# A two-layer graph network on one core: groups of 1,024 edges handled two at a time in the second layer and in the target scores of the first

## What is computed

```python
# layer 0 (per edge: src, dst; per head)
xl    = x @ W_lin.T
alpha = leaky_relu(xl[dst]*att_src + xl[src]*att_dst + (edge_attr_16 @ W_edge.T)*att_edge, 0.2)
e     = exp(alpha - segment_max(alpha, dst)[dst])
out   = segment_sum(xl[src] * e / segment_sum(e, dst)[dst], dst) + bias + x
x     = layernorm(x + elu(layernorm(out) * gamma + beta))
# layer 1
q, k, v = x @ Wq.T, x @ Wk.T, x @ Wv.T
alpha = sum_over_head(q[dst] * edge_attr_128 * k[src]) / sqrt(16) * edge_weight1
x     = layernorm(x + segment_sum(alpha * v[src], dst))
```

## Time and profile before

| what | us |
|---|---|
| median of 3 runs | 4161.83 (4160.66 to 4164.23) |
| the profiled execution | 4163.54 |
| its span, first to last instruction | 4161.8 |
| POOL busy | 3065.4 (74%) |
| DVE busy | 2682.8 (64%) |
| PE busy | 1924.6 (46%) |

### The profile page before, as it was taken

How to read it: one execution, slowest core, us unless ns; L and a number is a source line. 1 busy time by engine, 2 the same in 40 slices (tenths; PEclk the granted TensorE clock), 3 DMA queues, 4 the chain that set the end, 5 groups by cost and what they waited for, 6 DMA issues and landing times.

```text
span 4161.8 us, 47315 instructions
## 1 busy us (share of the span) xinstructions
PE 1924.6 (46%) x10576; PEld 1610.4 (39%) x10576; DVE 2682.8 (64%) x5083; ACT 256.5 (6%) x646; POOL 3065.4 (74%) x3247
## 2 busy tenths in 40 slices
PE   4644444554443454444534444444444444444444
PEld 2433333433332343333424444444444444444444
DVE  3555555655555566555657777777777777777776
ACT  1101101100111110001100000000000000000000
POOL 7777777777777777777447777777777777777775
PEclk6666667667666777766755555555555555555555
DMA  8444444444444444444257676666767767677674
GB/s 207 135 133 120 113 129 140 128 140 125 121 120 120 140 132 136 125 127 117 80 183 220 212 218 218 218 220 214 222 208 221 219 214 223 215 217 219 211 224 148
DMA packets 374070, 711.11 MB, mean 171 GB/s; under 512 B 129715, under 2 KB 217780, under 8 KB 373764
## 3 DMA queue, kind: packets, MB, share of 16 engines
q0 software_dynamic: 129504, 324.46, 28.8%
q1 hardware_dynamic: 198040, 354.75, 26.4%
q10 hardware_dynamic: 46476, 31.39, 2.4%
HBM read 682.18 MB, written 28.15 MB: 171 GB/s over the span
## 4 chain that ended last, share of the span: by engine, by line
POOL 37%; issue 21%; DVE 17%; DVEq 9%; PE 8%; DMA 5%; ACT 2%; POOLq 0%; SPq 0%; ACTq 0%
POOL ring L1326 23%; POOL ring L575 14%; DVEq L912 4%; DVE work L915 4%; DMA ring<-kv_table,den_cols 3%; PE psum L1352 3%; PE psum L697 2%; DVE psum L1468 1%; DVE ring L1466 1%; DVE psum L1463 1%; DVE ring L1477 1%; DVEq L73 1%; DMA dst_all<-dst_row_dram 1%; DVE work L1012 0%; DVE work L1015 0%
## 5 line engine op out<-in xcount | busy, mean ns | idle before, releaser
L575 POOL DMA_INDIRECT ring<-x_table,idx x1584 | 1501.0, 948 | 482.6 <-issue 459.7
L1326 POOL DMA_INDIRECT ring<-kv_table,den_cols x1516 | 1434.0, 946 | 462.1 <-issue 447.4
L1352 PE MATMUL psum<-work,ring 128*128 128x42 f32 x3232 | 735.3, 420 | 1093.0 <-DVE ring L1477 1093.0
L1352 PEld LDWEIGHTS psum<-work,ring 128*128 128x128 f32 x3232 | 704.5, 330 | 1148.6 <-DVE ring L1477 1148.6
L697 PE MATMUL psum<-work 128*42 128x132 f32 x3232 | 483.4, 312 | 201.5 <-DVE work L1015 201.4
L697 PEld LDWEIGHTS psum<-work 128*42 128x42 f32 x3232 | 407.0, 135 | 256.9 <-DVE work L1015 233.7
L1463 DVE TENSOR_TENSOR psum<-psum,ring 128x1024 f32<-128x1024 f32 x202 | 248.3, 1229 | 328.8 <-DMA ring<-kv_table,den_cols 304.0
L915 DVE TENSOR_TENSOR work<-dst_all,psum 126x1024 bf16<-126x1024 int32 x204 | 249.1, 1221 | 74.1 <-issue 42.9
L1453 DVE TENSOR_TENSOR work<-dst_all,psum 126x1024 bf16<-126x1024 int32 x202 | 246.7, 1221 | 77.8 <-issue 68.2
L1466 DVE TENSOR_TENSOR ring<-psum,ring 128x1024 f32<-128x1024 f32 x202 | 247.4, 1225 | 20.8 <-issue 9.5
L1468 DVE TENSOR_REDUCE psum<-ring 128x64 f32<-128x1024 f32 x202 | 247.9, 1227 | 14.8
(11 more groups left out here) (201 smaller groups left out, 2125.2 us busy)
## 6 DMA issues: line engine op xcount, KB each, us to landing
dst_all<-dst_row_dram SPq DMA_DIRECT2D x406, 512.0 KB, 5.7
ring<-ea_dram SPq DMA_DIRECT2D x202, 512.0 KB, 4.0
ring<-x_table,idx POOLq DMA_INDIRECT x1584
ring<-kv_table,den_cols POOLq DMA_INDIRECT x1516, 2.8
ea_pair<-ea_turned_dram SPq DMA_DIRECT2D x102, 128.0 KB
kv_table<-work ACTq DMA_DIRECT2D x17, 512.0 KB, 3.1
q_table<-work ACTq DMA_DIRECT2D x17, 384.0 KB, 3.9
ring<-q_table SPq DMA_DIRECT2D x202, 31.5 KB
```

Source lines behind the costliest of these rows:

```text
L575: pool.indirect_dma_start(x_rows[:, h * CHUNK_TILES + t, :], None, k["x_table"], bass.IndirectOffsetOnAxis(idx[h][:, t:t + 1], 0))\
L1326: pool.indirect_dma_start(kv[j][:, t, :], None, k["kv_table"], bass.IndirectOffsetOnAxis(index[:, tile:tile + 1], 0))\
L1352: last = pe.matmul(sum_ps[j % 2], message[j % 2][:, t, :], onehot[j][:, t, :], start=t == 0, stop=t == GROUP - 1)
```

## The change

Layer 0: `dst_all` of two buffers becomes one tensor `dst_pair`; one DMA loads 1 MB for two groups, one DVE instruction compares both, and the node numbers of all 12 groups of a chunk are made by one instruction ahead of the chunk (`first_nodes`). There is one such buffer and one `onehotT`, each for two groups.

Layer 1: all work goes in steps of two groups (16 tiles): DVE instructions over 2,048 columns, one wait for each two groups, three buffers of key/value rows of 16 tiles, two of `w` and `q_win`, one of `dst_pair`, `onehotT` and `q_ps`. The compare for two steps ahead stands after the messages, the adds of the step before stand between the products. Sums of a step are 16 matmuls; the two window bases are read once a chunk into registers.

```diff
-    dst_all = [sb(f"dst_all{i}", [P, GROUP * P], I32) for i in range(2)]
+    dst_pair = sb("dst_pair", [P, 2 * GROUP * P], I32)
+    dst_all = [dst_pair[:, i * GROUP * P:(i + 1) * GROUP * P] for i in range(2)]
...
-    onehotT = [part(GP // 2).bitcast(BF16)[0:KWIN, :] for _ in range(2)]
+    onehotT = part(GP).bitcast(BF16)[0:KWIN, :]
...
                         starts = window_starts(sp, regs, k["base_sb"], first_group, r)
+                        sp.wait_ge(onehotT_made, v + 1)
+                        sp.dma_start(dst_pair, k["dst_row"][0:1, bass.DynSlice(first_group * GP, 2 * GP)]
+                                     .to_broadcast([P, 2 * GP])).then_inc(dst_in, 16)
+                        sp.wait_ge(scores_added, v + 1)
                         for u in range(2):
-                            sp.wait_ge(dst_used, 2 * v + u + 1)
-                            sp.dma_start(dst_all[u], k["dst_row"][0:1, bass.DynSlice((first_group + u) * GP, GP)]
-                                         .to_broadcast([P, GP])).then_inc(dst_in[u], 16)
-                            sp.wait_ge(scores_added, 2 * v + u + 1)
                             sp.dma_start(ai_win[:, bass.DynSlice((4 * i + 2 * e + u) * (ROWS + HEADS0), HEADS0)],
                                          k["ai_table"][bass.DynSlice(starts[u], WIN), :, :].rearrange("n s h -> (n s) h"))\
-                              .then_inc(ai_in[u], 16)
+                              .then_inc(ai_in, 16)
...
         def scores_group(d, g):
-            pe.wait_ge(onehotT_made, d * CHUNK_GROUPS + g + 1)
-            pe.wait_ge(ai_in[g % 2], 16 * (d * HALF + g // 2 + 1))
+            u = g % 2
+            if u == 0:
+                pe.wait_ge(onehotT_made, d * HALF + g // 2 + 2)
+                pe.wait_ge(ai_in, 32 * (d * HALF + g // 2 + 1))
             for half in range(2):
                 last = pe.matmul(dst_ps[:, half * 512:(half + 1) * 512], ai_win[:, g * ROWS:(g + 1) * ROWS],
-                                 onehotT[g % 2][:, half * 512:(half + 1) * 512], start=False, stop=False)
-            last.then_inc(scores_added, 1)
+                                 onehotT[:, u * GP + half * 512:u * GP + (half + 1) * 512], start=False, stop=False)
+            if u:
+                last.then_inc(scores_added, 1)
...
-        for credit, n in ((rows_released, 2), (ea_used, 2), (dst_used, 2), (scores_added, 2), (runs_used, 1),
+        for credit, n in ((rows_released, 2), (ea_used, 2), (onehotT_made, 1), (scores_added, 1), (runs_used, 1),
...
+        def first_nodes(first_group):
+
+            dve.tensor_scalar(node_at, k["base_f"][0:KWIN, bass.DynSlice(first_group, CHUNK_GROUPS)],
+                              k["node_pass"][0:KWIN, :], None, ALU.add)
+
+        def scores_onehot(v, pair):
+
+            dve.wait_ge(dst_in, 16 * (v + 1))
+            dve.wait_ge(scores_added, v + 1)
+            dve.tensor_tensor(out=onehotT.rearrange("p (u c) -> p u c", u=2),
+                              in0=dst_pair.rearrange("p (u c) -> p u c", u=2)[0:KWIN, :, :],
+                              in1=node_at[:, bass.DynSlice(2 * pair, 2)].unsqueeze(2).to_broadcast([KWIN, 2, GP]),
                               op=ALU.is_equal).then_inc(onehotT_made, 1)
-            dve.drain().then_inc(dst_used, 1)
...
                     make(0, s, tile)
-                    scores_onehot(0, d, (s + 1) * CHUNK_GROUPS + 2 * g)
+                    scores_onehot(d, g)
+                    dve.drain()
                     if not first:
                         add(1, dve.snap(before, min_val=0, max_val=NODES), 2 * v - 1)
                     make(1, s, tile + GROUP)
-                    scores_onehot(1, d, (s + 1) * CHUNK_GROUPS + 2 * g + 1)
                     starts = window_starts(dve, regs, k["base_sb"], s * CHUNK_GROUPS + 2 * g, r)
                     dve.reg_mov(before, starts[1])
+                    dve.drain()
                     add(0, starts[0], 2 * v)
                     dve.reg_add(c_visit, c_visit, 1)
                     dve.reg_add(d_visit, d_visit, 1)
 
+                first_nodes((s + 1) * CHUNK_GROUPS)
+                dve.drain()
...
+            first_nodes(0)
+            dve.drain()
             with dve.Fori(0, HALF) as g:
                 v = dve.snap(d_visit)
-                for u in range(2):
-                    scores_onehot(u, v, 2 * g + u)
+                scores_onehot(v, g)
...
+    PAIR_TILES = 2 * GROUP
+    BUFS = 3
...
+        SUMS_DUE = 12
+
+        def pair(p):
+            n = pool.snap(done)
+            wait_here(pool, msg_made, n + p + MSG_CREDIT - BUFS + 1, pool_gate)
+            for t in range(PAIR_TILES):
+                if t == SUMS_DUE:
+                    wait_here(pool, summed, n + p + 2, pool_gate)
+                tile = p * PAIR_TILES + t
...
+        def sums(n, e):
+            pe.wait_ge(msg_made, n + MSG_CREDIT + 1)
+            for u in range(2):
+                for t in range(GROUP):
+                    last = pe.matmul(sum_ps[u], message[e][:, u * GROUP + t, :], onehot[e][:, u * GROUP + t, :],
+                                     start=t == 0, stop=t == GROUP - 1)
             last.then_inc(summed, 1)
...
+        def chunk(pairs, slot_due, last_chunk=False):
+            n = pe.snap(done)
+            for i in range(pairs):
+                if not last_chunk or i + 1 < pairs:
+                    pe.wait_ge(q_used, n + i + 3)
+                    spread((i + 1) % 2)
+                if slot_due and i == 0:
                     finish()
-            count_round(pe, counts, groups)
...
+            for i in range(pairs):
+                e, buf = i % 2, i % BUFS
+                group = CHUNK_GROUPS * c + 2 * i
+                sums_of = held if i == 0 else regs[2 * i - 2:2 * i]
+                adding = not (first_chunk and i == 0)
+                turn = dve.snap(due)
+
+                if last_chunk and i == pairs - 1:
+                    dve.wait_ge(last_kv_in, 16 * LAST_PAIR_TILES * (r + 1))
                 else:
-                    rows_in, rows_due = kv_in[j], 16 * GROUP * ((uses[j] if j < LAST_ROUND - 1 else uses[-1]) + 1)
-                messages(SLOTS * i + j, n0 + j, j, uses[j], rows_in, rows_due)
-                if slot_due and j == 1:
+                    dve.wait_ge(kv_in[buf], 16 * PAIR_TILES * ((long_uses if buf == 0 else short_uses) + i // BUFS + 1))
+                dve.wait_ge(q_spread, turn)
+                dve.tensor_tensor(out=tiles3(q_ps), in0=tiles3(q_ps), in1=kv[buf][:, :, 0:FEAT], op=ALU.mult)
+                if adding:
+                    dve.wait_ge(summed, turn)
+                    add(0, sums_of[0])
+                dve.drain()
+                dve.wait_ge(w_in[e], 16 * (even_odd[e] + i // 2 + 1))
+                dve.tensor_tensor(out=prod, in0=q_ps, in1=w[e], op=ALU.mult).then_inc(q_used, 1)
+                if adding:
+                    add(1, sums_of[1]).then_inc(added, 1)
+                dve.drain()
+                dve.tensor_reduce(out=alpha, in_=prod.rearrange("p (t d) -> p t d", d=FEAT // HEADS1), axis=AX.X, op=ALU.add)
+                if not last_chunk or i + 2 < pairs:
+                    make_node_at(group + 4)
+                dve.drain()
+                by_tile = alpha.rearrange("p (t h) -> p t h", h=HEADS1)
+                dve.scalar_tensor_tensor(
+                    out=by_tile, in0=by_tile, scalar=(FEAT // HEADS1) ** -0.5,
+                    in1=edge_w[:, bass.DynSlice(group * GROUP, PAIR_TILES)].unsqueeze(2).to_broadcast([P, PAIR_TILES, HEADS1]),
+                    op0=ALU.mult, op1=ALU.mult)
+                if not last_chunk or i + 1 < pairs:
+                    make_onehot(1 - e, group + 2)
+                dve.drain()
+                dve.tensor_tensor(
+                    out=message[e].rearrange("p t (h d) -> p t h d", h=HEADS1),
+                    in0=kv[buf][:, :, FEAT:].rearrange("p t (h d) -> p t h d", h=HEADS1),
+                    in1=by_tile.unsqueeze(3).to_broadcast([P, PAIR_TILES, HEADS1, FEAT // HEADS1]),
+                    op=ALU.mult).then_inc(msg_made, 1)
+                dve.reg_add(due, due, 1)
+                if not last_chunk or i + 2 < pairs:
+                    make_onehotT(e, even_odd[e] + i // 2 + 1, dve.snap(due))
+                if i == 0 and not first_chunk:
                     finish()
...
+            dve.wait_ge(summed, dve.snap(due))
+            add(0, held[0])
+            dve.drain()
+            add(1, held[1]).then_inc(added, 1)
```

337 lines of the change are left out of this document (141 added, 196 removed).

## The result

The changed kernel takes **4172.0 us** (median of 11 runs, 4168.8 to 4175.4) where the kernel before, on the same chip, takes 4161.8 (11 runs, 4159.1 to 4164.7): a ratio of **1.0023** (95% interval 1.0016 to 1.0031), 10.2 us slower. It lies in the range given, 4169 to 4204, at its low end: the sign is as forecast, the change less than half of the +22 forecast.

The account below looks back on a forecast made before the run. POOL's back-to-back issue of gathers was taken as the bound. Terms of 14.6 + 1.3 - 3.4 + 9.5 gave +22.0 us: 4185.5 on the profiled 4163.54, given as 4183.8 for the median, range 4169 to 4204.

Parts of the forecast that it names:

- The bound: Both layers: POOL issues gathers back to back, 3,224 at 1.25 us, 4,030 of 4,162 us; savings elsewhere are worth nothing.
- First pass of layer 0: Load and compare in series through one buffer, 9.0 us a step; POOL stands 14.6 us (6 to 24).
- Steady chunks: Layer 0's later chunks, steps of 8.5 us; the last messages cost +1.3 us (-1.8 to +10.5).
- The gathers' pace: POOL in both layers: gathers still 1.25 us apart.
- Node numbers once a chunk, drains: With fewer waits, these lie in DVE's slack or behind the load: nothing.
- Start of layer 1: POOL's one wait of 3.74 us for sums of the first groups goes: -3.4 us.
- Tail: End of layer 1: two groups in place of one behind the last gather, +9.5 us (8 to 11).
- change of layers: Between layers 0 and 1: output rows, their DMAs and `last_messages` as before.
- The covered pass: Rival: layer 0's first pass is hidden, its term is nothing: +7.4 us, 4169; chance 0.07.
- The chunk that starves: Rival: the single buffer starves every chunk of layer 0, 12.1 us a step: about +85 us, 4247; chance 0.07.
- Layer 1's own wait: Rival: in layer 1 the wait for sums holds POOL 1.5 us a chunk: +24 more, 4208; chance 0.04.
- the signs that I had named for being wrong: Loads of 1 MB under 5.5 or over 8 us, POOL gaps in later chunks, or a different pace of gathers.

Follow-up runs that it names:

- run 5: The changed kernel unaltered, on a chip where the kernel before takes 4985 us: 4984.3 us, 0.9995 of the kernel before.
- runs 16 to 18: Changed kernel again (4172.3 us), then with layer 1's last step split and cut and POOL's sums wait at the 8th (4162.3) or 4th tile (4163.3).
- runs 4, 6 and 17: Changed kernel, layer 1's last step group by group (0.9985); also second group cut (0.9976); cut plus POOL's sums wait at 8th tile (4162.3 us).
- run 2: Layer 0 of the changed kernel with layer 1 of the kernel before: 0.9986 of the kernel before.
- run 17: Changed kernel, layer 1's last step group by group and cut, POOL's wait for sums at the 8th tile, not the 12th: 4162.3 us, 1.0002.
- run 15: Changed kernel without POOL's wait for sums in layer 1: 5481 us, 1.0867 of the kernel before.
- run 14: Changed kernel with POOL's wait for sums in layer 1 at the 8th tile in place of the 12th: 5016 us, 0.9941 of the kernel before.
- run 13: Changed kernel with every compare of layer 0's first pass made three times over: 1.0031 of the kernel before.

## Why the prediction was right or wrong

**The bound: right, on a quick chip.** POOL issues without a pause in both layers, DVE's 169 us less bring nothing, and the time moves at the places named. On the late chips it doesn't hold: in run 5 POOL stands 98 times in layer 1, most often 4.64 us from gather to gather.

**First pass of layer 0: mechanism right, size wrong.** This is the step that failed: "I take 6.5" for a load of 1 MB. The trace has 56.99 to 63.14, 6.15 us, for the slowest, and 5.7 in the mean (8.1 - 2.3 - 0.2 by the step); in runs 16 to 18 the steps are 7.8, 7.5 and 7.9, so 5.0 to 5.4. Five steps at 9.0 in place of 8.1 are 4.3 us, and the first compare began at 54.53, not 55.3. The 14.6 us are 9.5, and 5.6 to 7.4 in the other three executions. POOL was held at tile 8, where the cover is 0.9 us, for the 1.2 that I read at tile 12. The 6.5 are the 4.8 of the half and the 1.6 to 2.1 us that I took for 512 KB more; measured, these were 0.9 in the mean. The other load that the change makes twice as large, edge features in layer 1, went from 4.0 us in the median to 5.5:

```profile
ring<-ea_dram SPq DMA_DIRECT2D x101, 1024.0 KB, 5.5
```

There the same bytes cost 1.5, so the slope isn't one number either. The Trainium skill, page "DMA: Bandwidth & Descriptors", section "Anatomy of one DMA", gives 1 us for each 436 KB, for DMAs issued from POOL. Taken over to these, which SP issues, it makes an estimate of 1.2 us for 512 KB more, between the 0.9 and the 1.5 measured; 4.8 + 1.2 = 6.0 would have been nearer than 6.5. I had set the page's line aside because its whole figure for 512 KB was too low.

**Steady chunks: wrong sign.** + 1.3 forecast, - 2.7 measured. This isn't the load. I had followed the chain to compares ending 4.3, 15.9, 24.5 ... 50.1 us after the start, and 55.9 in all; they end 4.3, 12.2, 20.7 ... 46.6, and 52.2 in all. From the second to the last it is 34.4 us, for 34.2 forecast, so the step of 8.5 was right (measured 7.9 to 8.9, with waits of 0.9 to 1.2 us for the load or up to 1.7 for TensorE's scores). What failed is the second compare: it waits for TensorE's scores, as I said, but these were there 9.7 us after the start (the row at 1971.47 waited 0.15 us for them), and I had them some 3.7 later. The term lies 0.9 us outside its bounds (-1.8 to +10.5), which allowed for the load alone.

**The gathers' pace: not foreseen.** Between POOL's release and layer 0's last gather the four executions of the new layer 0 take 1893.6 to 1894.5 us, the one of the old 1896.2. In layer 1, from first to last gather, the four take 2013.6 to 2014.0, the old one 2018.4, of which 3.4 is the wait. That is 1.8 to 2.6 and 1.0 to 1.4 us won. Of the kernel before on a quick chip there is one profiled execution, so that the change won them is likely, not shown; I had written "gathers still 1.25 us apart" and didn't look for 0.1%.

**Node numbers once a chunk, drains: right**, as far as can be seen: L913 puts 0.4 us ahead of the last `messages` (1961.56 to 1961.99), inside the term above. They weren't tried apart.

**Start of layer 1: right**, - 3.4: no gap in any of the four.

**Tail: right**, + 8.3 for + 9.5. The step before the last messages ended earlier than placed: DVE waited 0.18 us for its sums, not 1.1. It is also what runs 4, 6 and 17 moved by the amounts worked out.

Together: 22.0 - 5.1 (first pass) - 4.0 (messages) - 2.2 - 1.4 (pace) - 1.2 (tail) + 0.5 (change of layers) = 8.6.

**The rivals.** The covered pass (4169) is the nearest number, for another reason: there was a hold. The low bounds of all parts add up to + 8.8, so the measured + 10.2 lies at their very edge. Nearly all misses went the same way, and that the time is still inside the range is luck in part. The chunk that starves wasn't seen. Layer 1's own wait is there on the late chips, but the old layer 1 has it as well: pauses of over 1 us add up to 389 us in 112 in run 2, and to 368 in 98 in run 5. Of the signs that I had named for being wrong two came: loads under 5.5 us (5.2 in the first pass, and less in the later executions), and a pace of the gathers that differs.

**What a late chip makes of it.** Tail + 22 us (47.2 for 25.2), layer 1's steps - 20.4 (2352.0 for 2372.4), POOL's release in layer 0 some 6 earlier: - 4 by these terms, of which the time shows - 1 (0.9995, no difference).

**A better version.** On the quick chip none ran faster than the kernel before; run 17 brings the changed one level with it. On late chips the cut tail (0.9976) and the pause at the 8th tile (0.9941) beat both. The mended first pass together with the cut tail should take 4153 to 4157 us on a quick chip: run 17's 4162.3 less the 5.8 to 9.5 us by which POOL was let go late. That remains an estimate, since it ran only on late ones.

## What to carry to other kernels

Where one engine's issue bounds a kernel, a larger step elsewhere is paid for at the ends: at the start by the first loads put in series, at the tail by the work that now stands behind the last landing. The tail's part was had back by a small last step (run 17); the start's should be by small first loads, which wasn't tried where it counts. Such a tail can be worked out from a timeline to about a microsecond (+ 9.5 for + 8.3 ahead of the change, - 5.5 for - 5.4 and - 9.5 for - 10.0 with its trace at hand). For the price of a larger transfer take a measured one of the smaller size and give the slope for the bytes a range: here 512 KB more cost 0.9 us in one place and 1.5 in another. And where a step waits for two things, follow both; the wait that was misplaced here was the one for TensorE, and its term had bounds for the load alone.

## What the runs showed of the hardware that I had not expected

- The same kernel takes 4162 us in two measurements and 4983 to 5038 on five other chips, each within 0.7%, with the same granted clock in layer 1 (0.50 in run 5 as in the changed kernel's first profile). What sets the two kinds apart wasn't found.
- On the latter, TensorE's work becomes known late when POOL has issued many gathers since its last pause: DVE's add comes 14.6 us behind the start of 32 matmuls whose rows span 7.05 where 12 or 13 gathers have been issued (run 5), 30 us behind it where there are 18 (run 15), and 7.2 us where there are 6 (run 15, POOL issuing) or POOL is done (run 5's tail). Without the pause in a step the kernel takes 5481 us.
- Taking seven eighths of the sums' matmuls away wins 0.7% of the kernel before there.
- SP suffers too: two DMAs of `q_table` take 2.10 us of its queue in run 5 and 0.90 on the quick chip.
- A kernel that pauses its gathers for a wait can therefore be faster than one that doesn't; on a late chip four tiles' difference in where it pauses is worth some 30 us of 5040 (22.6 in layer 1's gathers and 8.9 in the tail, run 14 against run 13).
